# Attention products of the first four output tiles inside the last attention batch, and products four tiles ahead

## The chip, the cores and the metric

One core of a Trainium2 chip. The metric is the device time of one execution, in microseconds (us); three executions of the kernel before took 1540.43, 1540.65 and 1542.9 us.

## The reference

```python
x = L0_attn_x                                   # (8, 512, 1024) float32
x = x + layernorm(attention(layernorm(x)))      # 8 heads of 64, w_qkv, w_o
x = x + layernorm(ffn(layernorm(x)))

def attention(x):
    q, k, v = split(x @ w_qkv.T + b_qkv)
    scores = where(causal, einsum('bhfc,bhtc->bhft', k, q), -10000.0)
    vals = einsum('bhft,bhfc->bhtc', softmax(scores, axis=-2), v)
    return vals @ w_o.T + b_o

def ffn(x):                                     # dense layer and one of four LoRA ranks per row
    scores = x @ gate_w.T + gate_b              # ranks 8, 16, 32, 64; the best one is taken
    return x @ W.T + b + (x @ A[:r].T) @ B[:, :r].T
```

Every product is float32-exact in the kernel: each operand is split into a high part and a rest (names ending in h and l), and three TensorE passes stand for one.

## The kernel before, in words

**Attention phase** (`attention_phase`, L78 to L1143). A loop over the first seven batches of 512 rows, and the last batch written out by the same function with `last=True`. Each batch runs through ten slots (`body`). Slot h has projections of q, k or v after the tables `BETWEEN` and `BETWEEN_LAST` (L105, L118), the scores of head h, the spread of the masked weights of head h-1, the transposes of its probabilities, and the values of head h-2. All engines follow such a slot in their own order, by hand. ACT makes the exponentials and the high parts, DVE the maximum (`scores_max`, L607), the low parts (`p_lo`, L577) and the sum of the values (`vals_sum`, L633), POOL the denominator, the diagonal WT (L461) and the normalised probabilities (`normalise`, L465). SP stores each head's values to memory (`store_vals`, L349); `vals_sum` waits for the store of the head before, since there is one buffer. In the last batch no next batch's projections exist. From slot 5 on, SP loads the output phase's weights: wo (4 chunks), B, wag (8 chunks of 1092 columns); each is split into high (`next_high`, ACT) and low part (`next_low`, DVE; L532, POOL). In slots 8 and 9 TensorE makes the product of output tile 0 (`first_output`, L1069). Its y (`first_attention_out`, L651), scale (L537) and normalised z (L880) follow.

**Output phase** (`output_phase`, L1146 to L1573). A second block with its own semaphores, whose starting values memsets on POOL give (L1308 to L1317). It begins with the product of tile 1, the six wag splits that are left (`late`), the residual x1 and the second layernorm of tile 0, the transposes of its x2n and its x2T parts. Then a loop over the batches, four tiles of 128 rows each. Per tile n on TensorE (L1557): `ffn(n)` (72 matmuls of 364 columns in three banks, the transpose of the routing's result `us` inside the last, 6 matmuls with B), `transpose_x2(n+1)`, `attention_product(n+2)` (24 matmuls of 512 columns; none after the last two tiles). `ffn(n+1)` waits until the three banks of tile n are read (`f_done`, L1534). DVE (L1407): y and statistics of tile n+1, the routing of tile n (L1349, ten small operations), the values' low part, statistics of x1, the low part of x2T, f out of the banks and its statistics. POOL (L1299): scale of y, x1 = x + z (`first_residual`), scale of x1, scale of f, outs = x1 + zf (`second_residual`), all of them in this order. ACT (L1482): the values' high part, z, uT, x2n, x2T's high part, zf.

The few lines on which the order in the output phase rests:

```python
ffn(n)                                   # TensorE, L1560
if more:
    transpose_x2(n + 1)
if not (last and i + 2 > 3):
    attention_product(b, i + 2)
...
layernorm_scale(0, 4 * b + i + 1)        # POOL, L1302
first_residual(b, i + 1)
layernorm_scale(1, 4 * b + i + 1)
layernorm_scale(2, 4 * b + i)
second_residual(b, i)
```

Of the kernel before, what the change touches and what calls it, by code (L numbers as in the profile page):

```python
# [23 lines left out]
P = 128  # L24
# [4 lines left out]
class OutputWeights:  # L29

    def __init__(self, nc, ctx, NB, S, D, PART, R, NAG):
        def sb(name, shape, dt, c=ctx):
            return c.enter_context(nc.sbuf_tensor(name, shape, dt))

        KD, KV = D // P, PART // P
        self.R, self.KV = R, KV
        self.SPLIT_EARLY = 7

        with ExitStack() as early:
            wag_raw = sb("wag_raw", [P, KD, NAG], F32, early)
            wo_raw = sb("wo_raw", [P, KV, D], F32, early)
            B_raw = sb("B_raw", [P, D], F32, early)
        self.wagl = sb("wagl", [P, KD, NAG], F32R)
        self.wol = sb("wol", [P, KV, D], F32R)
        self.Bl = sb("Bl", [P, D], F32R)
        self.wagh = sb("wagh", [P, KD, NAG], F32R)
        self.woh = sb("woh", [P, KV, D], F32R)
        self.Bh = sb("Bh", [P, D], F32R)  # L50
        self.vraw = sb("vraw", [P, 2, PART // P, P], F32)
        self.vh = sb("vh", [P, 2, PART // P, P], F32R)
        self.vl = sb("vl", [P, 2, PART // P, P], F32R)
        self.bo_s = sb("bo_s", [P, D], F32)
        self.y = sb("y", [P, D], F32)
        self.z = sb("z", [P, D], F32)
        self.stats = sb("stats2", [P, 3, 12], F32)
        self.mv = sb("mv2", [P, 3, 2], F32)
        self.var_eps = sb("var_eps2", [P, 3], F32)
        self.rstd = sb("rstd2", [P, 3], F32)  # L60
        self.shift = sb("shift", [P, 3], F32)
        self.xs = sb("xt", [P, 2, D], F32)
        self.floats = 2 * (D // P * NAG + PART // P * D + D) + 3 * 2 * PART + 5 * D
        self.floats += 5 * 64

        self.chunks = [("wo", k, wo_raw[:, k, :], self.woh[:, k, :], self.wol[:, k, :]) for k in range(KV)]
        self.chunks += [("B", 0, B_raw[:, :], self.Bh[:, :], self.Bl[:, :])]
        self.chunks += [("wag", k, wag_raw[:, k, :], self.wagh[:, k, :], self.wagl[:, k, :]) for k in range(KD)]
# [8 lines left out]

def attention_phase(nc, x, wqkvT, bqk, bv, valsT, wl_late, vals_stored, ps_o, W, woT, bo, wagT, BT):  # L78

# [38 lines left out]
    BETWEEN_LAST = BETWEEN[:2] + [([(kind, p, 0, FIRST)], [(kind, p, 0, SECOND)])  # L118
                                  for kind, p in (("k", 2), ("q", 2), ("k", 3), ("q", 3))] + 4 * [([], [])]
# [17 lines left out]
    with ExitStack() as ctx:  # L137
# [6 lines left out]
        wh = sb("wh", [P, KD, E], F32R)  # L144
        wl = sb("wl", [P, KD, 2 * PART], F32R)
# [3 lines left out]
        wl_v_late = sb("wl_v_late", [P, KD - KEPT, PART], F32R)  # L149
        xTh = sb("xTh", [P, KD, S], F32R)  # L150
        xTl = sb("xTl", [P, KD, S], F32R)
        xs = sb("xs", [P, 3, D], F32)

        assert W.floats - D <= 2 * KD * (E + S) + 3 * D
        qst = sb("qst", [P, 2, 2, S], F32R)
        kst = sb("kst", [P, 2, 2, 2, S], F32R)

# [11 lines left out]
        ident = sb("ident", [P, P], F32)  # L169
# [10 lines left out]
        mhalf = sb("mhalf", [P, 1], F32)  # L180
        mone = sb("mone", [P, 1], F32)
        eps = sb("eps", [P, 1], F32)
        hold = sb("hold", [1, 5], F32)
# [67 lines left out]
        tiles_landed = sem("tiles_landed")  # L251
        v_first_landed = sem("v_first_landed")
        v_first_hi = sem("v_first_hi")
        v_first_lo = sem("v_first_lo")
        first_out = sem("first_out")
        first_mv = sem("first_mv")
        first_scale = sem("first_scale")

        LOADS = {5: range(0, 4), 6: range(4, 8), 7: range(8, 11), 8: range(11, 13)}
        SPLITS = {6: range(0, 2), 7: range(2, 4)}
        POOL_SPLITS = range(4, W.SPLIT_EARLY)

        xf = x.rearrange("b s d -> (b s) d")
        vf = valsT.rearrange("b c t -> (b c) t")


        W_CHUNKS = [[k] for k in range(KD)] + [[k, k + 1] for k in range(0, KD, 2)]

        def wh_chunk(n):

            ks = W_CHUNKS[n]
            return wh[:, ks[0], 0:2 * PART] if len(ks) == 1 else wh[:, ks[0]:ks[0] + 2, 2 * PART:3 * PART]
# [51 lines left out]
        def turned(h, place, last):  # L326

            half = None if last else TURNED.get(h, [None] * 3)[place]
            return [] if half is None else [half]

        def between(h, part, b, last):

            return [(kind, p, b + ahead, ks) for kind, p, ahead, ks in (BETWEEN_LAST if last else BETWEEN)[h][part]]

# [3 lines left out]
        def _(sp):  # L338
# [4 lines left out]
            def dup_k(p, b):  # L343

                sp.wait_ge(k_low, 4 * b + p + 1)
                sp.dma_start(kst[HD:P, p % 2, 0, :, :].bitcast(F32), kst[0:HD, p % 2, 0, :, :].bitcast(F32)).then_inc(k_dup[p % 2], 16)
                sp.dma_start(kst[0:HD, p % 2, 1, :, :].bitcast(F32), kst[HD:P, p % 2, 1, :, :].bitcast(F32)).then_inc(k_dup[p % 2], 16)
# [14 lines left out]
            def body(b, last):  # L362
                if not last:

                    sp.wait_ge(k_full, 4 * b + 1)
                    for t in range(3):
                        load_x(t, b + 1)
                for h in range(SLOTS):
                    if h == 2 and not last:

                        sp.wait_ge(v_full, 4 * b + 4)
                        load_x(3, b + 1)
                    if h in (3, 5):
                        dup_k((h + 1) // 2, b)
                    if h in (7, 9) and not last:
# [3 lines left out]
                    if h == 6 and not last:  # L379
# [3 lines left out]
                    if last and h == 5:  # L383
# [1231 lines left out]
```

## Time and profile before

| | |
|---|---|
| median of three executions | 1540.65 us |
| the profiled execution, its own time | 1543.97 us |
| its span, first to last instruction | 1542.1 us |
| busy: PE, DVE, ACT, POOL | 97%, 64%, 45%, 41% |
| mean granted TensorE clock | 0.983 |

A busy share is the time in which an engine had an instruction in work; matmuls overlap one another, so that the distance of two starts tells what one costs. The granted clock is the share of TensorE's full speed that the chip gave in the stretch. Of the span, the attention phase is the first 884 us and the output phase the rest.

### The profile page before, as it was taken

Reading aid. Unit: us, or ns where it says so; the run is one execution under the profiler, and the core shown is the slowest. Engines: PE = TensorE matmul, PEld = TensorE weight load, DVE = VectorE, ACT = ScalarE, POOL = GpSimd, SP = SyncE. Lnnn points to the kernel's source line nnn. Section 1 sums busy time; section 2 is a strip of 40 time slices with the busy share of each in tenths; the row PEclk is TensorE's granted clock in tenths of the full one; section 3 lists DMA queues with packets and bytes.
Section 4 is the critical chain, followed back from the end, with each engine's and each line's share of the span. In section 5 each row is a group of like instructions: output and inputs, shape, how many; then the busy total and the mean of one; then the engine's idle time right before and its main releaser. Section 6 shows DMA issues by size and latency. Waiting matters only on the chain. (4 is left out here: it accounts for less than half of the span.)

```text
span 1542.1 us, 24973 instructions
## 1 busy us (share of the span) xinstructions
PE 1489.6 (97%) x8032; PEld 1313.2 (85%) x8032; DVE 982.4 (64%) x2105; ACT 700.7 (45%) x1499; POOL 626.9 (41%) x1162
## 2 busy tenths in 40 slices
PE   7999999999999999999998689999999999999996
PEld 5888888888888888888887579999999999999996
DVE  7576575664765756756746666666666666666663
ACT  5374474563654655646635633333333333333332
POOL 2253361452543615524513523434444444433433
PEclk9999999999999999999999789999999999999998
DMA  6212113122121131121202612222212222211111
GB/s 232 83 38 82 49 29 90 34 54 75 37 54 61 37 95 34 43 73 37 54 18 73 221 43 69 69 68 68 68 68 68 68 68 68 68 59 56 58 58 41
DMA packets 46926, 102.92 MB, mean 67 GB/s; under 512 B 5040, under 2 KB 21424, under 8 KB 46896
## 3 DMA queue, kind: packets, MB, share of 16 engines
q1 hardware_dynamic: 46896, 102.54, 21.4%
q8 instruction: 16, 0.26, 0.1%
q14 instruction: 14, 0.11, 0.0%
HBM read 60.06 MB, written 25.69 MB: 56 GB/s over the span
## 5 line engine op out<-in xcount | busy, mean ns | idle before, releaser
L1539 PE MATMUL ps_f<-wagh,x2Th 128*128 128x364 f32 x768 | 256.4, 334 | 4.4 <-DVE f L1401 2.9
L1539 PE MATMUL ps_f<-wagl,x2Th 128*128 128x364 f32 x768 | 253.6, 330 | 0.0
L1539 PE MATMUL ps_f<-wagh,x2Tl 128*128 128x364 f32 x768 | 253.1, 330 | 0.0
L973 PE MATMUL ps_o<-xTh,wh 128*128 128x512 f32 x504 | 207.0, 411 | 2.9 <-DVE xTl L562 2.9
L973 PE MATMUL ps_o<-xTh,wl 128*128 128x512 f32 x504 | 198.6, 394 | 0.0
L973 PE MATMUL ps_o<-xTl,wh 128*128 128x512 f32 x504 | 197.8, 392 | 0.0
L1539 PEld LDWEIGHTS ps_f<-wagh,x2Th 128*128 128x128 f32 x768 | 145.5, 189 | 7.2 <-issue 5.0
L1539 PEld LDWEIGHTS ps_f<-wagl,x2Th 128*128 128x128 f32 x768 | 145.5, 189 | 1.3
L1539 PEld LDWEIGHTS ps_f<-wagh,x2Tl 128*128 128x128 f32 x768 | 145.4, 189 | 0.0
L1272 POOL TENSOR_TENSOR var_eps<-mv,eps 128x1 f32<-128x1 f32 x95 | 19.3, 203 | 301.4 <-DVE mv L1335 301.4
L446 POOL TENSOR_TENSOR cw<-wm,cnt 128x4 f32<-128x4 f32 x64 | 12.9, 201 | 307.5 <-ACT pr L808 307.5
L470 POOL TENSOR_SCALAR pr<-pr,rden 128x128 f32<-128x128 f32 (+3 forms) x256 | 137.2, 555 | 0.0
L808 ACT ACTIVATE pr<-ps_s,nm 128x128 f32<-128x128 f32 (+3 forms) x256 | 130.6, 521 | 0.1
L580 DVE TENSOR_TENSOR PTl<-ps_t,PTh 128x512 fp32r<-128x512 f32 (+1 forms) x192 | 110.4, 599 | 23.0 <-ACT PTh L775 19.8
L1440 ACT ACTIVATE zf<-f,shift,rstd 128x512 f32<-128x512 f32 x64 | 48.7, 808 | 164.0 <-POOL shift L1276 164.0
L1386 DVE TENSOR_TENSOR x2Tl<-ps_x,x2Th 128x512 fp32r<-128x512 f32 x64 | 43.8, 692 | 119.2 <-ACT x2Th L1460 118.8
L973 PEld LDWEIGHTS ps_o<-xTh,wl 128*128 128x128 f32 x504 | 95.3, 189 | 21.5
L973 PEld LDWEIGHTS ps_o<-xTh,wh 128*128 128x128 f32 x504 | 95.5, 190 | 19.8 <-DVE xTl L562 3.1
L973 PEld LDWEIGHTS ps_o<-xTl,wh 128*128 128x128 f32 x504 | 95.8, 190 | 17.1
L622 DVE TENSOR_REDUCE nm<-ps_s 128x1 f32<-128x128 f32 (+3 forms) x256 | 107.8, 484 | 2.2
L1518 PE MATMUL ps_o<-woh,vh 128*128 128x512 f32 x248 | 101.3, 408 | 3.9 <-POOL hold L1317 3.9
L775 ACT ACTIVATE PTh<-ps_t 128x512 fp32r<-128x512 f32 (+1 forms) x192 | 94.4, 527 | 21.9 <-PE ps_t L1047 19.9
(175 smaller groups left out, 3527.6 us busy)
## 6 DMA issues: line engine op xcount, KB each, us to landing
kst<-kst SPq DMA_DIRECT2D x64, 256.0 KB, 3.6
xt<-in_x SPq DMA_DIRECT2D x32, 512.0 KB, 4.0
out<-outs SPq DMA_DIRECT2D x32, 512.0 KB, 3.0
xs<-in_x SPq DMA_DIRECT2D x24, 512.0 KB, 4.3
valsT<-vt SPq DMA_DIRECT2D x64, 128.0 KB, 2.3
vraw<-valsT SPq DMA_DIRECT2D x32, 256.0 KB, 4.1
raw<-in_wqkvT SPq DMA_DIRECT2D x12, 512.0 KB, 6.1
wag_raw<-in_wagT SPq DMA_DIRECT2D x8, 546.0 KB, 5.2
```

The source lines that it names most:

```text
L446: pool.tensor_tensor(cw[:, q, :], wm[:, q, :], cnt[:, :], ALU.mult).then_inc(cw_done, 1)
L470: last = pool.tensor_scalar(at, at, rden[:, q, i:i + 1], 1.0, ALU.mult, ALU.mult)
L580: dve.tensor_tensor(PTl[:, o:o + n], ps_t[g % 2][:, 0:n], PTh[:, o:o + n].bitcast(F32), ALU.subtract).then_inc(t_lo, 1)
L622: last = dve.tensor_reduce(nm[:, q, i:i + 1], ps_s[:, S_OFF[i]:S_OFF[i] + (i + 1) * P], AX.X, ALU.max, negate=True)
L775: act.activation(PTh[:, o:o + n], ps_t[g % 2][:, 0:n], ACT.Copy).then_inc(t_hi, 1)
L808: last = act.activation(pr[:, q, S_OFF[i]:S_OFF[i] + n], ps_s[:, S_OFF[i]:S_OFF[i] + n], ACT.Exp, bias=nm[:, q, i:i + 1], accum_out=acc[:, ...
L973: done = pe.matmul(ps[:, :], w[:, k, c:c + P], xT[:, k, :], start=(k == 0 and w is wh and xT is xTh), stop=(k == KD - 1 and w is wl), skip ...
L1272: pool.tensor_tensor(var_eps[:, c:c + 1], mv[:, c, 1:2], eps[:, :], ALU.add)
L1386: dve.tensor_tensor(x2Tl[:, 4 * g:4 * g + 4, :], ps_x[:, g, :].rearrange("p (k t) -> p k t", k=4), x2Th[:, 4 * g:4 * g + 4, :].bitcast(F32 ...
L1440: return act.activation(out_, in_, ACT.Identity, scale=rstd[:, c:c + 1], bias=shift[:, c:c + 1])
L1518: last = pe.matmul(ps_o[:, half, :], a[:, i % 2, k, :], w[:, k, cols], start=(k == 0 and a is vh and w is woh), stop=(k == KV - 1 and a is ...
L1539: last = pe.matmul(ps_f[:, g, 0:GW], a[:, k, :], w[:, k, cols], start=(k == 0 and a is x2Th and w is wagh), stop=False, skip_group_check=True)
```

## The change

The attention phase gets `last_body` functions for every engine, an order by hand for the last batch, in place of `body(NB - 1, True)`:

- the projections of the last batch end in slot 4; slots 5 to 8 hold the attention products of output tiles 0 to 3 (`tile_product`), in the two banks that the projections used;
- y and its statistics for tiles 0 to 2 (`tile_out`), scale, z, x1, second layernorm, transposes and x2T of tile 0 all lie in slots 5 to 9; so do all splits of wo, wag and B;
- the loads of the weights go out earlier: wo after the last v projection, wag, B, bo after the last q projection;
- the memory places of weights and tiles are laid out anew for that, and the semaphores of the output phase exist from the start, with starting values set by POOL at the head of the last batch.

In the output phase TensorE makes the product of tile n+4, DVE y of tile n+3, POOL the scale of y of tile n+3, ACT z of tile n+1 at the head of a tile; y has four buffers. No product stands in the last batch. The opening part of the phase is gone.

```diff
+            def last_body(b):                       # SP
+                sp.wait_ge(v_full, 4 * b + 4)
+                for n in range(W.KV):
+                    load_next(n)
+                for n in range(2):
+                    load_vals(n)
...
+                store_vals(2, b)
+                sp.wait_ge(q_full, 4 * b + 4)
+                sp.dma_start(W.bo_s[:, :], bo.partition_broadcast(P)).then_inc(W.bo_landed, 16)
+                for n in W.wag:
+                    load_next(n)
+                load_next(W.B)
+                sp.wait_ge(s_done, 8 * b + 6)
+                sp.dma_start(W.xs[0][:, :], xf[0:P, :]).then_inc(W.x_landed[0], 16)
+                for h in range(3, NH):
+                    store_vals(h, b)
...
+                for h in range(NH):                 # POOL
+                    if h == 6:
+                        next_low(W.wag[0])
+                        next_low(W.wag[1])
+                        tile_scale(0, 0, 0)
+                    elif h == 7:
+                        tile_residual()
+                        next_low(W.wag[2])
+                    denominator(h, b)
+                    weights(h, b)
+                    diagonal(h, b)
+                    normalise(h, b)
+                tile_scale(1, 4, 0)
+                tile_scale(0, 1, 1)
+                for k in (4, 5, 7):
+                    next_low(W.wag[k])
+                tile_scale(0, 2, 2)
...
+                scores_max(7, b)                    # DVE, slots 7 and 8
+                tile_out(1, 1)
+                tile_vals_low(3)
+                reciprocal(7, b)
+                p_lo(6, 0, b)
+                p_lo(6, 1, b)
+                vals_sum(5, b)
+                tile_statistics()
+                tile_out(2, 0)
+                p_lo(6, 2, b)
+
+                tile_out(2, 1)
+                next_low(W.wag[3])
+                p_lo(7, 0, b)
+                p_lo(7, 1, b)
+                vals_sum(6, b)
+                next_low(W.wag[6])
+                p_lo(7, 2, b)
+                tile_low()
+                next_low(W.B)
+                vals_sum(7, b)
...
+            def tile_product(n, half, ks):          # TensorE
+                if ks[0] == 0:
+                    pe.wait_ge(W.v_ready, n + 1)
+                    if n == 0:
+                        pe.wait_ge(next_lo, W.KV)
+                        pe.wait_ge((k_low, q_low)[half], 4 * NB)
+                    else:
+                        pe.wait_ge(W.y_done, 2 * n - 1 + half)
...
+                for h in range(NH + 1):
+                    if h < len(BETWEEN_LAST):
+                        steps(h, 0, b, True)
+                    else:
+                        tile_product(h - 5, 0, whole)
+                        masked_weights(h - 1, b)
+                    if h >= 2:
+                        values(h - 2, b)
+                    if h >= 1:
+                        transpose_p(h - 1, 0, b)
+                        transpose_p(h - 1, 1, b)
+                    if h < len(BETWEEN_LAST):
+                        steps(h, 1, b, True)
+                    elif h < NH:
+                        tile_product(h - 5, 1, whole)
+                    if h + 1 < NH:
+                        scores(h + 1, b)
+                    if h == NH:
+                        transpose_tile()
+                    if h >= 1:
+                        transpose_p(h - 1, 2, b)
+                tile_product(3, 1, first)
+                values(NH - 1, b)
+                tile_product(3, 1, second)
...
             def body(b, last):                      # output phase, POOL
                 for i in range(4):
                     if not (last and i == 3):
-                        layernorm_scale(0, 4 * b + i + 1)
                         first_residual(b, i + 1)
-                        layernorm_scale(1, 4 * b + i + 1)
-                    layernorm_scale(2, 4 * b + i)
+                    if not (last and i + AHEAD - 1 > 3):
+                        layernorm_scale(0, b, i + AHEAD - 1)
+                    if not (last and i == 3):
+                        layernorm_scale(1, b, i + 1)
+                    layernorm_scale(2, b, i)
                     second_residual(b, i)
...
                     ffn(n)                          # output phase, TensorE
                     if more:
                         transpose_x2(n + 1)
-                    if not (last and i + 2 > 3):
-                        attention_product(b, i + 2)
+                    if not last:
+                        attention_product(b, i + AHEAD)
...
-            attention_product(0, 1)
-            pe.wait_ge(consts, 5)
-            transpose_x2(0)
-            pe.wait_ge(w_ready, len(late))
```

## Rows read from the trace of the kernel before

**Rows 1.** Stretches: start:end, length, each engine's busy us (instructions), granted clock, DMA.
```profile
801.20:840.60 39.40, 38.15 (x207) 32.39 (x205) 23.58 (x56) 22.70 (x61) 10.84 (x26) 1.00 0.15 38
840.60:901.00 60.40, 37.33 (x152) 29.93 (x152) 40.02 (x60) 32.82 (x58) 30.17 (x52) 0.75 0.57 189
901.00:922.50 21.50, 21.50 (x112) 20.37 (x112) 12.61 (x32) 4.35 (x7) 5.31 (x10) 0.90 0.00 1
922.50:1460.00 537.50, 536.04 (x2998) 493.41 (x2997) 352.58 (x811) 177.17 (x270) 218.72 (x351) 1.00 0.20 66
1460.00:1516.90 56.90, 53.87 (x311) 50.37 (x310) 35.68 (x86) 19.06 (x29) 23.52 (x37) 0.99 0.15 51
```

**Rows 2.** Waits of PE, 740 to 960 us: waiting, releaser, total, times, longest.
```profile
PE ps_x L1528 <- ACT x2n L1440: 5.4, 1, 5.4
...
PE ps_o L1518 <- POOL hold L1317: 3.9, 1, 3.9
```

**Rows 3.** Timeline of PE, slot 2: start, duration, engine, line, operation, tiles, shapes, count.
```profile
801.24 0.39 PE L973 MATMUL ps_o<-xTh,wh 128*128 128x512 f32 x1
...
804.14 0.40 PE L1062 MATMUL ps_v<-PTh,v 128*128 128x512 f32 x1
...
805.82 1.04 PE L1047 MATMUL ps_t<-ident,pr 128*128 128x128 f32 x8
...
810.96 0.40 PE L973 MATMUL ps_o<-xTh,wh 128*128 128x512 f32 x1
```

**Rows 4.** Timeline of DVE, 847 to 879 us.
```profile
847.10 0.62 DVE L617 COPY_PREDICATED_SCALAR ps_s<-maskf,masked 128x384 f32 x1
...
849.73 0.17 DVE L627 TENSOR_SCALAR nm<-nm 128x3 f32<-128x3 f32 x1
...
856.10 2.44 DVE L644 TENSOR_TENSOR wol<-wo_raw,woh 128x1024 fp32r<-128x1024 f32 x2
...
877.25 0.68 DVE L657 TENSOR_TENSOR y<-ps_o,bo_s 128x512 f32<-128x512 f32 x1
878.01 0.70 DVE L659 BATCH_NORM_STATS2 stats<-y 128x6 f32<-128x512 f32 x1
```

**Rows 5.** Timeline of POOL, 843 to 882 us.
```profile
843.80 2.06 POOL L470 TENSOR_SCALAR pr<-pr,rden 128x128 f32<-128x128 f32 x4
...
855.07 5.05 POOL L470 TENSOR_SCALAR pr<-pr,rden 128x128 f32<-128x128 f32 x4
...
876.39 5.03 POOL L535 TENSOR_TENSOR wagl<-wag_raw,wagh 128x1092 fp32r<-128x1092 f32 x2
```

**Rows 6.** DMA issues, 838 to 905 us: KB each, median us to landing.
```profile
wo_raw<-in_woT SPq DMA_DIRECT2D x4, 512.0 KB, 7.1
...
valsT<-vt SPq DMA_DIRECT2D x5, 128.0 KB, 2.3
```

**Rows 7.** Timeline of ACT, the uT copies of tiles 0 and 1.
```profile
914.29 0.28 ACT L1473 ACTIVATE uT<-ps_u 128x128 fp32r<-128x128 f32 x1 [7.37 <-PE ps_u L1545]
...
933.78 0.28 ACT L1473 ACTIVATE uT<-ps_u 128x128 fp32r<-128x128 f32 x1 [4.36 <-PE ps_u L1545]
```

**Rows 8.** Timeline of POOL, tile 29: outs and x1.
```profile
1481.23 2.54 POOL L1296 TENSOR_TENSOR outs<-x,zf 128x512 f32<-128x512 f32 x2 [1.00 <-ACT zf L1440]
...
1486.05 2.53 POOL L1287 TENSOR_TENSOR x<-xt,z 128x512 f32<-128x512 f32 x2 [1.00 <-ACT z L1440]
```

**Rows 9.** Timeline of DVE, the routing of tile 0.
```profile
907.22 0.16 DVE L1356 TENSOR_TENSOR scores<-ps_f,gb_s 128x4 f32<-128x4 f32 x1 [3.34 <-PE ps_f L1539]
...
907.70 1.17 DVE L1361 TENSOR_TENSOR tmax<-pmax,scores 128x1 f32<-128x1 f32 x1
...
910.71 0.23 DVE L1374 TENSOR_TENSOR us<-um,us 128x64 fp32r<-128x64 f32 x1
```

**Rows 10.** Timeline of PE, between the last two tiles.
```profile
1512.92 1.03 PE L1528 MATMUL ps_x<-ident,x2n 128*128 128x128 f32 x8
1516.88 0.64 PE L1539 MATMUL ps_f<-wagh,x2Th 128*128 128x364 f32 x1 [2.93 <-DVE f L1401]
```

More of the change, by code:

```diff
@@ L420, in _ @@
             with sp.Fori(0, NB - 1) as b:
[L421 to L425 removed]
+                body(b)
+            last_body(NB - 1)
         @block.gpsimd
@@ L665, in lows, with body @@
+            def lows(h, part, b):
+                for kind, p, row, ks in between(BETWEEN, h, part, b):
                     if ks is not FIRST:
                         {"q": q_lo, "k": k_lo, "v": v_lo}[kind](p, row)
-            def body(b, last):
+            def body(b):
                 for h in range(SLOTS):
-                    if h < NH and (h != BARE + 1 or last):
+                    if h < NH and h != BARE + 1:
                         scores_max(h, b)
-                    if 1 <= h <= 3 and not last:
+                    if 1 <= h <= 3:
@@ L682, in body @@
-                    if h in (BARE, BARE + 1) and not last:
+                    if h in (BARE, BARE + 1):
                         reciprocal(h, b)
@@ L687, in body @@
                         p_lo(h - 1, 1, b)
-                    elif h == BARE + 1 and not last:
+                    elif h == BARE + 1:
                         p_lo(h - 1, 0, b)
@@ new lines, in tile_norm, with tile_high @@
+            def tile_norm(out_, in_, c, row, done):
+                act.wait_ge(W.ln_ready[c], 1)
+                for half in range(2):
+                    cols = slice(PART * half, PART * half + PART)
+                    act.activation(out_[:, cols], in_[:, cols], ACT.Identity, scale=W.rstd[row], bias=W.shift[row])\
+                        .then_inc(done, 1)
+            def tile_high():
+                for g in range(2):
+                    act.wait_ge(W.x2_full, 2 + g + 1)
+                    act.activation(W.x2Th[:, 4 * g:4 * g + 4, :],
+                                   ps_s[:, 512 * g:512 * g + 512].rearrange("p (k t) -> p k t", k=4), ACT.Copy)\
+                        .then_inc(W.x2_hi, 1)
@@ L1009, in scores @@
                     pe.wait_ge(exp_done, H)
-                if h == BEHIND and not last:
+                if behind:
                     pe.wait_ge(x_raw, 8 * b + 5)
@@ L1083, in step, with steps @@
                     project(kind, p, row, ks, last)
-            def steps(h, part, b, last):
-                for n, (kind, p, row, ks) in enumerate(between(h, part, b, last)):
+            def steps(h, part, b, last=False):
+                for n, (kind, p, row, ks) in enumerate(between(BETWEEN_LAST if last else BETWEEN, h, part, b)):
                     here = n == 0 and part == 0 and 1 <= h <= NH and (h != BARE or last)
```

787 lines of the change are left out of this document (455 added, 332 removed).

## The prediction

> **What bounds the kernel now.** I read the page first, then stretches of it cut at the borders of the work, then what TensorE waited for, then the engines' timelines around those waits. TensorE is the bound: in a slot of the attention phase and in an output tile it hardly idles. The exception is the crossing between the phases. From 840.6 to 901.0 us it is busy 37.3 of 60.4 us and its granted clock is 0.75, so part of that time runs at 1.2 instead of 2.4 GHz [rows 1]. In that stretch the projections are used up: heads 6 and 7 alone don't fill TensorE, and then come the end of the block, the second phase's constants, one residual and one layernorm in a row. The longest waits there are 5.4 us for the normalised tile and 3.9 us for the memsets at the start of the second phase [rows 2].
>
> The second thing to see is a small one in each output tile. 27 tiles take 537.5 us [rows 1], 19.91 each, while tiles 0 to 1 are 19.49 apart by their uT copies [rows 7]. No matmul is slower; the two transposes of x2n come late by 0.4 us. Their loop through the other engines takes as long as the period: f out of PSUM, its layernorm, outs, then on POOL the next tile's scale and x1, then its layernorm.
>
> **Step 1, slots 2 to 4 of the last batch.** The same 96 projection matmuls now stand as 36, 36 and 24, where they were 24 in each of slots 2 to 5. Twelve with the mask's matmul take 2.90 us (801.24 to 804.14), so 2.72 without it (384 of its columns against 12 x 512); a whole slot with 24 takes 9.72 (801.24 to 810.96) [rows 3]. So the slots take 12.4 + 12.4 + 9.7 = 34.6 us, and slot 5 begins at 801.2 + 34.6 = 835.8. The splits of wo on ACT and DVE (2.44 us for two on DVE [rows 4]) lie beside them: DVE was busy 23.6 of 39.4 us there [rows 1]. I cost the loads of wo, wag and x at nothing while slots 4 and 5 cover them; see the store in step 2.
>
> **Step 2, slots 5 to 8.** Each gets 24 product matmuls of 512 columns, the work of a projection slot: 9.7 us by TensorE alone, so slot 8 would begin at 864.9. But products 1 to 3 overwrite the bank of the one before, and wait for its y. That add stands on DVE behind a full head. DVE's slot: maximum of the scores 2.8 (847.10 to 849.90), y and statistics of two halves 2 x 1.45 and an aggregate of 0.2, the values' low part 0.6 (half of a wo split), the rest of the head 1.7 (the mean 23.6 / 4 = 5.9 of slots 2 to 5, less the maximum and less 1.4 for a split of q or k, which I put at two operations like y's 0.68): 8.2 us busy [rows 1, 4]. It also waits about 2 us for exps and denominators, so some 10.3 us against 9.7. Slot 7 has the statistics of x1 on top, 2 x 0.7 us. And the store of head 3's values is issued behind about 6 MB of weights; a store lands in 2.3 us, but the four 0.5 MB pieces of wo, issued in a row, took 7.1 [rows 6], so some 0.3 MB per us. Six MB from 835 on need 20 us: the store lands near 856, where DVE wants the buffer at 854. Following the orders of DVE, ACT and POOL I get products 1, 2 and 3 begun late by 0.3, 2.4 and 3.5 us, the third at 869.6. From there TensorE has 2.72 + 0.2 + 1.68 (values, 804.14 to 805.82) + 1.0 (ten transposes) + 0.8 (x2n's eight; 1.04 with the tail) + 2.72 + 1.68 = 10.8 us [rows 3], and waits some 1.7 us for p_lo of head 7, which on DVE stands behind two splits of wag: 882.2. POOL is as late: its normalise of 2.06 us took 5.05 beside DVE splits [rows 5], and after it come two scales of about 1.3 (the 2.3 us between two residuals in [rows 8], less 1 of waiting for z), three splits of 2.5 (5.03 for two [rows 5]) and a third scale: 883.3. The border of the blocks I put at 0.7 us, an estimate well below the wait of 3.9 [rows 2], which also held the end of tile 0's first layernorm and the memsets; both are now inside the last batch. So the first output matmul comes at 884 instead of 901.0, with nothing left ahead of it: **17.0 us**. Bounds: 877.5 if TensorE never waits (864.9 + 10.8 + 1.8 for the last store and the border), 890 if POOL's normalise takes 5 us twice more. I take 884, as DVE's sum is known from rows.
>
> **Step 3, half clock in tile 0.** 901.0 to 922.5 is 21.5 us where an undisturbed tile is 19.49 [rows 1, 7]: 2.0 lost. Before it TensorE had idled 5.4 and 1.5 us; now some 2. Between 0 and 2.0 I take half: **1.0 us**.
>
> **Step 4, products four tiles ahead.** z and the scale of tile n+1 are now ready a tile early. On POOL x1 follows outs at once; before, outs ended at 1483.77 and x1 began at 1486.05 [rows 8], with a scale and the wait for z between. That takes 2.3 us out of a loop of 19.91. It moves x1 onto the routing on DVE, ten small operations: one with two SBUF inputs took 1.17 us beside x1 at 907.70, against 0.16 of the one at 907.22 [rows 9]. With x1's halves of 1.27 us I expect one or two such holds, 1.0 to 1.5 us, as long as the loop passes there. 19.91 - 2.3 + 1.5 = 19.1, under the 19.49 of TensorE, which then sets the pace: 27 x 0.42 = **11.3 us**. Bounds: 0, and 11.3.
>
> The Trainium skill ("SBUF — State Buffer", "Who interferes with whom") says that a VectorE instruction with two SBUF inputs and a GpSimd instruction that reads SBUF block each other for the whole instruction, whichever issued first. By that, the trace agrees: 1.17 us in place of 0.16. Taken at its worst (each routing operation that meets x1 or a scale is held) step 4 would give nothing; that is rival B.
>
> **Step 5, the last tiles.** Now the last four tiles are followed by no product, where it was the last two. Without one, f of tile n must leave its banks before tile n+1 starts: 3.96 us from the transposes to the first matmul (1512.92 to 1516.88, idle 2.93 [rows 10]), and two more such gaps appear. The loop sets the distance of the transposes: 19.91 - 2.3, plus about 1 for the holds and the clock, 18.5. From the start of tile 28 to that of tile 31: 13.2 (19.49 less 2 x 2.75 of the product and 0.8 of transposes) + 18.5 + 18.5 + 4.0 = 54.2, against 56.9 [rows 1]: **2.7 us**. So of the 11.0 us of two products taken out here, 8.3 come back as waits. Bounds: 0 (loop as before) and 5.3 (17.2 by TensorE alone).
>
> **The rest** costs nothing: keep's one memset, the other places of tiles, the transposes of tile 0 moved (in step 2).
>
> **Sum.** 17.0 + 1.0 + 11.3 + 2.7 = 32.0 us. The profiled execution took 1543.97 us, 1542.1 of them span, 3.3 above the median of 1540.65. Its own time less the sum is 1512.0; the median less the sum is **1508.7 us**, which I give.
>
> **Rivals.**
> B: the tile's period stays at 19.9, as the holds on the routing give back the 2.3 us, or another wait has it. For: DVE is busy 352.6 of 537.5 us there [rows 1], and the routing is in the loop. Against: 1.5 us of holds leave 0.4 of margin. Steps 1 to 3 and 5 remain, 20.7 us: 1520.
> C: slots 5 to 8 are bound by DVE and POOL worse than I follow: softmax, y, wag and layernorm feed one another in order, and a slot of 12 us in place of 10.3 to 11 puts the first output matmul at 890 or more. Step 4 stays: 1515 to 1518; with B, 1528.
> D: the crossing goes as TensorE's own sum says (877.5) at full clock: 6.5 and 1.0 us more, with some of step 5's: 1499.
> E, slower than before: the routing, under x1, hands over its result (the tile named us) too late. TensorE transposes that inside the tile, 11.0 us after its start (922.5; its uT copy at 933.78 [rows 1, 7]). The routing begins when 24 of 72 matmuls are done, 4 us into the tile, and took 3.7 us with one hold, 907.22 to 910.94 [rows 9]: it ends at about 8. Further holds beyond 3 us make TensorE wait inside the tile, 31 times; the point from which all 32 us are lost is 1.03 us each, so 4.0 us of holds, three to four of 1.17. At 4.2 us: 1546. Against: x1 has two halves, and each can hold DVE once.
> That the change does not do what it says I exclude by the text of both phases: tile 0's x2 is complete in the first.
>
> The skill ("DMA: Bandwidth & Descriptors", "Queues, rings and completion order") says that each engine takes the descriptors of a ring in order. Only the burst's 7.1 us bear on it here; if the store passed the weights, product 2 would come 1.3 us sooner, less than a term of the range.
>
> **How the numbers follow.** Forecast 0.50; B 0.20; C 0.14, D 0.12, E 0.03; the crossing's gain lost by some unseen wait, 0.01. The forecast's own width is 6 each way, from the bounds of steps 2 and 5. Low end 1498 takes in D; high end 1524 takes in B and most of C; left out are C with B, E, and a little under D. A change of 0.2% (3 us) is about what a measurement here can tell from none. Only E and part of an extreme C fall there: faster 0.95, same 0.02, slower 0.03.
>
> **What would show it.** The first output matmul at 884 with an idle of about 2 us before it; products 2 and 3 waiting for y on DVE by 2 to 4 us; the store of head 3's values landing near 856; clock above 0.9 from 840 to 884. uT copies 19.5 us apart, transposes of x2n without idle before them, the operations of the routing held by x1. Three idle stretches of about 3 us before first matmuls at the end, where there was one. It is wrong if the uT copies stay 19.9 apart (B), if product 3 starts after 876 (C), or if idle time appears before the transpose of that result (E).

## The result, and the profile after

The changed kernel took 1527.03 us (median of 4, 1526.36 to 1529.8) beside 1541.27 us (1540.43 to 1542.9) for the kernel before on the same chip: a ratio of 0.991 (95% interval 0.9893 to 0.9927), 14.2 us. Predicted were 1508.7 us and a range of 1498 to 1524. The change is faster, by less than half of what was forecast, and the time lies 3 us over the range.

The profiled execution has a span of 1525.0 us, 17.1 less than the one of before. Here are its stretches, cut at the same events of the work as [rows 1]: start:end, length, busy us of PE, PEld, DVE, ACT and POOL (instructions), granted clock, DMA share, GB/s.

```profile
801.20:836.90 35.70, 34.69 (x186) 29.64 (x185) 25.40 (x50) 23.69 (x55) 13.28 (x22) 1.00 0.36 107
836.90:896.40 59.50, 44.21 (x223) 36.93 (x221) 43.39 (x74) 33.22 (x69) 36.14 (x47) 0.91 0.41 128
896.40:918.40 22.00, 19.97 (x112) 18.46 (x113) 11.84 (x32) 4.91 (x8) 5.28 (x10) 1.00 0.27 86
918.40:1446.00 527.60, 527.60 (x3000) 495.65 (x2999) 342.76 (x811) 173.31 (x270) 218.43 (x352) 1.00 0.19 67
1446.00:1499.75 53.75, 44.19 (x262) 42.78 (x260) 30.16 (x74) 17.50 (x27) 21.33 (x31) 0.97 0.14 49
1499.75:1525.00 25.25, 14.81 (x79) 14.49 (x79) 6.47 (x22) 3.32 (x5) 7.03 (x10) 0.79 0.10 42
```

Set against the stretches of before, with one correction: the traces of this record differ by some 2 us before DVE's first maximum of the first head (47.3 us in before's, 46.2 in this one), so that piece is taken out.

| stretch | before | after | gain | predicted |
|---|---|---|---|---|
| start to the first scores | 47.3 | 46.2 | 1.1 | 0 |
| first scores to the first output matmul | 853.7 | 850.2 | 3.5 | 17.0 |
| tile 0 | 21.5 | 22.0 | -0.5 | 1.0 |
| tiles 1 to 27 | 537.5 | 527.6 | 9.9 | 11.3 |
| tiles 28 to 30 | 56.9 | 53.75 | 3.1 | 2.7 |
| the last tile to the end | 25.2 | 25.25 | 0.0 | 0 |

The output tiles did what was forecast. 13.5 of the 14.9 us that are missing in the sum are missing in the second line, the crossing. In the fifth stretch, TensorE idles 9.6 of 53.75 us; that is the price of having no product there.

TensorE's waits from 740 to 960 us (waiting, releaser, total, times, longest), against [rows 2]:

```profile
PE ps_o L1351 <- DVE y L747: 9.3, 3, 6.8
PE ps_v L1333 <- DVE PTl L670: 3.5, 1, 3.5
PE ps_x L1785 <- ACT x2n L1708: 2.0, 1, 2.0
PE ps_f L1796 <- PEq L192: 1.6, 1, 1.6
...
```

The wait of 5.4 us for the normalised tile is down to one of 2.0 in the next tile, and the one of 3.9 us for the memsets is gone. Others have come in their place. In the timeline of PE, those of the crossing are the idle times in brackets at the second product half of slot 5, products 2 and 3, the values of head 7 and the first output matmul:

```profile
843.41 0.47 PE L1351 MATMUL ps_o<-woh,vh 128*128 128x512 f32 x1 [0.78 <-DVE qst L677]
865.15 0.77 PE L1351 MATMUL ps_o<-woh,vh 128*128 128x512 f32 x1 [6.84 <-DVE y L747]
878.01 0.47 PE L1351 MATMUL ps_o<-woh,vh 128*128 128x512 f32 x1 [2.21 <-DVE y L747]
890.06 0.80 PE L1333 MATMUL ps_v<-PTh,v 128*128 128x512 f32 x1 [3.50 <-DVE PTl L670]
896.40 0.43 PE L1796 MATMUL ps_f<-wagh,x2Th 128*128 128x364 f32 x1 [1.57 <-PEq L192]
```

A first matmul of 0.77 or 0.80 us instead of 0.47 says one more thing: after the two longest idle times TensorE starts at the lower clock. Of the twelve matmuls from 865.15 on, those from 865.71 to 869.12 start 0.43 us apart, and from 869.45 on they start 0.23 apart again, as at full clock. This half of product 2 takes 4.8 us where one at full clock takes 2.8.

What DVE did meanwhile, in its timeline:

```profile
851.46 1.65 DVE L717 TENSOR_SCALAR nm<-nm 128x3 f32<-128x3 f32 x1
...
863.54 0.74 DVE L728 SCALAR_TENSOR_TENSOR vt<-ps_v,bv_s,vt 64x512 f32<-64x512 f32 x1 [5.22 <-DMA valsT<-vt]
...
880.56 3.10 DVE L734 TENSOR_TENSOR wagl<-wag_raw,wagh 128x1092 fp32r<-128x1092 f32 x1
...
886.08 3.59 DVE L734 TENSOR_TENSOR wagl<-wag_raw,wagh 128x1092 fp32r<-128x1092 f32 x1
...
901.76 0.69 DVE L1622 TENSOR_TENSOR y<-ps_o,bo_s 128x512 f32<-128x512 f32 x1 [6.90 <-DMA gb_s<-in_gb]
```

DVE waits 5.22 us for the store of head 3's values to free its buffer; y of product 1 and so product 2 stand behind it. An operation on 128 by 3 numbers takes 1.65 us where [rows 4] have 0.17. Two splits of wag take 3.10 and 3.59 us, where two of the slightly smaller wo took 2.44 together. And y at the head of the output phase waits 6.90 us for the gate's bias.

SP's queue shows why the store is late: it is issued behind the weights (issue time, duration, count of DMAs):

```profile
834.70 4.03 SPq L404 DMA_DIRECT2D vraw<-valsT  x2
...
839.96 4.50 SPq L401 DMA_DIRECT2D wag_raw<-in_wagT  x8
844.50 1.14 SPq L398 DMA_DIRECT2D B_raw<-in_BT  x2
...
846.98 0.52 SPq L392 DMA_DIRECT2D valsT<-vt  x1
```

### The profile page after: what moved, and what is told of

Its sections match the earlier page's. It is cut to its first block and busy times, and to the rows that moved or that the text cites. A ratio compares the mean times of both kernels' runs of the same rounds, so it can differ in the third digit from the quotient of the medians.

```text
span 1525.0 us, 25023 instructions
## 1 busy us (share of the span) xinstructions
PE 1474.4 (97%) x8032; PEld 1310.3 (86%) x8032; DVE 971.0 (64%) x2103; ACT 696.8 (46%) x1501; POOL 631.7 (41%) x1155
## 3 DMA queue, kind: packets, MB, share of 16 engines
q1 hardware_dynamic: 46896, 102.54, 21.6%
## 5 line engine op out<-in xcount | busy, mean ns | idle before, releaser
L1565 POOL TENSOR_TENSOR small<-small,eps 128x1 f32<-128x1 f32 x92 | 17.4, 190 | 304.8 <-DVE small L1614 304.8
L1708 ACT ACTIVATE zf<-f,small 128x512 f32<-128x512 f32 x64 | 48.7, 809 | 164.6 <-POOL small L1569 164.6
L1740 ACT ACTIVATE uT<-ps_u 128x128 fp32r<-128x128 f32 x32 | 8.9, 277 | 237.7 <-PE ps_u L1802 237.7
L1665 DVE TENSOR_TENSOR x2Tl<-ps_x,x2Th 128x512 fp32r<-128x512 f32 x62 | 40.2, 687 | 119.1 <-ACT x2Th L1729 119.1
```

The source lines that it names most:

```text
L1665: dve.tensor_tensor(x2Tl[:, 4 * g:4 * g + 4, :], ps_x[:, g, :].rearrange("p (k t) -> p k t", k=4), x2Th[:, 4 * g:4 * g + 4, :].bitcast(F32 ...
L1708: return act.activation(out_, in_, ACT.Identity, scale=rstd[r], bias=shift[r])
```

## Experiments

Eleven kernels ran, all edits of the changed kernel. Medians are of four executions where nothing else is said; the kernel before took 1543.12 us beside the first four, 1541.46 beside the next four and 1540.91 beside the last three. Ratios are to these. The changed kernel ran beside 1541.27 us, so a difference in us to it can be off by up to 1.9 us from that source, and a comparison of ratios is the safer one.

**1. The store ahead of the weights.**

```diff
-                for n in W.wag:
+                for n in W.wag[:3]:
                     load_next(n)
-                load_next(W.B)
...
                 for h in range(3, NH):
                     store_vals(h, b)
+                    if h == 3:
+                        for n in W.wag[3:]:
+                            load_next(n)
+                        load_next(W.B)
```

> Edit: only the order on the SP queue. The last five wag chunks and B are loaded after the store of head 3's values instead of before it. Theory Q (the store stands behind six MB of weights): DVE's wait of 5.2 us before the sum of head 4's values is under 0.5 us, product 2 starts near 858 instead of 865.15 and at full clock, the first output matmul comes 7 to 9 us earlier than 896.4; time near 1519. Theory D (DVE's own work is what delays the products): product 2 still starts after 862, time above 1524.

Measured: 1521.89 us, ratio 0.9871 (0.9852 to 0.9889). DVE's wait for the store is gone. TensorE's timeline:

```profile
860.03 0.47 PE L1354 MATMUL ps_o<-woh,vh 128*128 128x512 f32 x1 [1.62 <-DVE y L750]
...
872.85 0.47 PE L1354 MATMUL ps_o<-woh,vh 128*128 128x512 f32 x1 [3.18 <-DVE y L750]
```

Product 2 comes 5.1 us earlier, product 3 5.2, the first output matmul at 889.81 instead of 896.40. So the queue was 5 to 6.5 us of the missing 13.5. It was not all: ahead of product 3 TensorE still waits, 3.18 us here, and DVE's timeline of this kernel shows two holds of the operation on 128 by 3 on the way there:

```profile
851.95 1.22 DVE L720 TENSOR_SCALAR nm<-nm 128x3 f32<-128x3 f32 x1
...
863.54 1.92 DVE L720 TENSOR_SCALAR nm<-nm 128x3 f32<-128x3 f32 x1
```

Both start while POOL splits wag (848.11 for 5.04 us, two in a row, and 862.89 for 2.54) and end at 853.17 and 865.46, when POOL's split in work ends (853.15 and 865.43).

**2. The wait for the bias inside the routing.** One line, `dve.wait_ge(bias_landed, 32)`, moved from ahead of the output phase's loop to the first operation that reads the bias.

> Edit: only the place of DVE's wait for the output phase's two bias loads, which stands ahead of the loop's first y and moves into the routing. Theory W (that wait makes y, routing and x2n of tile 1 late): DVE's idle of 6.9 us at 895 to 902 is gone, TensorE's idle of 2.0 us before the transposes of tile 1 is gone, time 1525. Rival X (the load of x for tile 1, landed at 899.5, sets the end of that chain): y comes earlier but the idle before the transposes stays above 1 us, time 1526.5 to 1527.

Measured: 1524.41 us, 0.9885 (0.9866 to 0.9904). That interval overlaps the changed kernel's, so the trace decides: tile 1's uT copy comes 19.41 us after tile 0's (905.75 to 925.16), where the changed kernel needs 21.84 (907.77 to 929.61), and the wait of 2.0 us ahead of tile 1's transposes is gone. So 2.4 us of tile 0's loss came from one wait placed too early. The clock in tile 0 is 1.00 in both; step 3's reason, half clock, was not what kept the tile long.

**3. The last low part of head 7's probabilities ahead of a split of wag.** On DVE, `p_lo(7, 2, b)` and `next_low(W.wag[6])` change places.

> Edit: only the order on DVE in slot 8; the last low part of head 7's probabilities comes before the split of wag chunk 6 instead of behind it. Theory P (TensorE's wait of 3.5 us before the last values is the path): values of head 7 start near 887 instead of 890.06, and first output matmul moves with it by 3.5 to 4.3 us, time near 1523. Rival L (DVE's splits, held by POOL's three splits to 3.1 and 3.6 us where 1.2 is their length, set the end of the block, whichever comes first): values start near 887, but DVE still ends near 894 and the first output matmul comes only about 1 us earlier, time 1526.

Measured: 1525.42 us, 0.989 (0.9872 to 0.9908), an interval that overlaps the changed kernel's. The wait of the values of head 7 falls from 3.50 to 0.41 us, and 2.5 us of it return at the border:

```profile
886.92 0.51 PE L1333 MATMUL ps_v<-PTh,v 128*128 128x512 f32 x1 [0.41 <-DVE PTl L670]
894.32 0.67 PE L1796 MATMUL ps_f<-wagh,x2Th 128*128 128x364 f32 x1 [4.05 <-PEq L192]
```

DVE's split that was passed still stands ahead of B's and of the last sum of values, and the second phase begins after all of them. The crossing, from the first product matmul to the first output matmul, takes 57.3 us here. That shows no gain: kernels 2, 4 and 5, where this code is untouched, took 57.7, 57.3 and 59.0 us, and the changed kernel 59.5. Changing places inside a queue whose sum is the bound gained nothing that these traces can tell from their spread.

**4. The loop's old order.** POOL's scale of y again ahead of x1, and ACT's z waiting for that scale; everything else as changed.

> Edit: in the output loop alone, POOL makes the scale of the far tile before x1 again, and ACT makes z only when that scale is done; product, y and buffers stay four and three tiles ahead. Theory S (the loop through POOL sets the old period of 19.9 us): the distance of the uT copies goes from 19.53 back to 19.9, 26 tiles lose 9.7 us, and the last tiles some more; time 1537 to 1541. Rival T (the period fell for another reason, such as the memory places or the products' distance): the copies stay 19.5 apart and the time stays at 1527.

Measured: 1536.8 us (ten executions, 1533.38 to 1540.94), 0.9966 (0.9953 to 0.9978). 23 periods from 950.14 to 1405.54 are 19.80 us each. The changed kernel has 19.53, that of before 19.91. So 0.27 of the 0.38 us that a period had gained come back with the old order, which makes the order of POOL and the early z the larger part of step 4's gain; what holds the other 0.11 is open. In time it is 9.8 us by the medians and 8.6 by the ratios. The ten executions spread over 7.6 us, and the profiled one is the fastest of them, only 6.4 us above the changed kernel's.

**5. f out of the banks first.** On DVE, f is added out of its three banks ahead of the low part of the next x2T.

```diff
                         second_layernorm(b, i + 1)
+                    ffn_add(b, i)
+                    if more:
                         x2_low(n + 1)
                     ffn_out(b, i)
```

> The changed kernel with one move on DVE: f is added out of its three banks before the low part of the next tile's x2T, not after it; nothing else. In the last batch, where no product stands between the tiles, the three first ffn matmuls waited 2.92, 2.82 and 2.76 us for f out of the banks. If the low part of x2T that stands ahead of f on DVE is part of that wait (about 1.3 us), each of the three waits falls to some 1.5 us and the stretch from the first matmul of tile 28 to that of tile 31 from 53.8 to about 50 us; over the rest the period stays at 19.53 us, since there f has the whole product to leave the banks. If the low part gates the first matmul as much as f does (it is an operand of it), the wait changes its name only and the time stays within 1 us. The crossing is the same code in both cases: first output matmul at 894 to 897.

Measured: 1517.31 us (1517.0 to 1521.09), 0.9854 (0.9837 to 0.9872): 9.7 us under the changed kernel (8.6 by the ratios), where I had expected about 3.8. More than half was foreseen, the gaps at the end:

```profile
1457.38 0.43 PE L1800 MATMUL ps_f<-wagh,x2Th 128*128 128x364 f32 x1 [1.57 <-DVE x2Tl L1665]
```

The other two are 1.41 us each. In the changed kernel the three are twice as long:

```profile
1462.75 0.41 PE L1796 MATMUL ps_f<-wagh,x2Th 128*128 128x364 f32 x1 [2.92 <-DVE f L1681]
...
1481.35 0.40 PE L1796 MATMUL ps_f<-wagh,x2Th 128*128 128x364 f32 x1 [2.82 <-DVE f L1681]
...
1499.75 0.41 PE L1796 MATMUL ps_f<-wagh,x2Th 128*128 128x364 f32 x1 [2.76 <-DVE f L1681]
```

From the uT copy of tile 28 to that of tile 31, the changed kernel takes 55.61 us and this one 50.16: 5.45 gained. f is out of the banks by the time TensorE has done the transposes (1455.7 and 1455.8); in the changed kernel it was 2.8 us behind them (1462.6 and 1459.8). Its statistics, outs, x1 and the next x2n come earlier with it. The other part was not foreseen: the period itself. The uT copies of tiles 1 and 27, first in the changed kernel, then in this one:

```profile
929.61 0.28 ACT L1740 ACTIVATE uT<-ps_u 128x128 fp32r<-128x128 f32 x1 [7.35 <-PE ps_u L1802]
...
1437.45 0.28 ACT L1740 ACTIVATE uT<-ps_u 128x128 fp32r<-128x128 f32 x1 [7.35 <-PE ps_u L1802]
```

```profile
928.86 0.28 ACT L1744 ACTIVATE uT<-ps_u 128x128 fp32r<-128x128 f32 x1 [8.63 <-PE ps_u L1806]
...
1433.61 0.28 ACT L1744 ACTIVATE uT<-ps_u 128x128 fp32r<-128x128 f32 x1 [8.56 <-PE ps_u L1806]
```

26 periods are 507.84 us there, 19.53 each, and 504.75 here, 19.41: 3.1 us. From the first of the eight transposes of x2n to the product, the changed kernel takes 0.87 to 1.04 us (in before it was 1.04 to 1.12), this one 0.79 in every period. So x2n's second half was still a little late. No wait is listed for it, as the first transpose was on time.

**6 and 7. All four edits, and then the best order.** Kernel 6 has edits 1, 2, 3 and 5. Kernel 7 has also POOL's split of wag 4 in slot 7 in place of the end of the batch, and on DVE `tile_out(2, 0)` ahead of `tile_statistics()`.

> Four edits in one: the loads of wag 3 to 7 and B behind the store of head 3's values (alone: 5 to 6 us), the wait for the gate's bias inside the first routing and not ahead of the loop (2 to 3 us), the last low part of head 7's probabilities ahead of the split of wag 6 on DVE (1 to 2 us), and f out of the banks ahead of x2T's low part (0 to 3 us). If these waits were independent losses the sum is 8 to 13 us under the changed kernel: 1514 to 1519, with the first output matmul at 887 to 889 and tile 1's uT copy 19.5 after tile 0's. If POOL and DVE behind each other are the real limit of the crossing (rival), the edits overlap: the first output matmul stays at 889 to 890, as with the store alone, and the time is 1518 to 1521.

Measured for kernel 6: 1511.4 us (1511.01 to 1512.31), 0.9811 (0.9795 to 0.9827), 15.6 us under the changed kernel. The four edits alone gained 5.1, 2.6, 1.6 and 9.7 us, 19.0 in sum, so 3.4 us are shared; by the ratios it is 21.6 in sum against 15.3. The rival's place for the first output matmul held, and the time was still under the first range, as edit 5 had gained more than I had allowed it. The first output matmul is at 890.47, where the store alone had 889.81, so in the crossing the other edits add nothing to the store; the border has a wait of 2.46 us.

> The kernel of the four edits, with POOL's split of wag 4 moved from the end of the last batch to slot 7, and y's first half of tile 2 on DVE ahead of the statistics of x1. If three splits on POOL at the end, 8.6 us of them beside two on DVE (3.1 and 2.0 to 3.6 us each in place of 1.2), are what holds B's split and so the border, the first output matmul comes 1.5 to 2.5 us earlier than in the kernel of four edits, and product 2 begins without the wait for y (1.6 us): 1512 to 1517. If slots 5 to 8 are bound by POOL itself (rival), the split in slot 7 pushes the denominator and the normalised probabilities of head 7 by 2.5 us, the products come later by that, and the time is the same or 1 to 2 us worse.

Measured for kernel 7: 1509.68 us (1508.09 to 1511.29), 0.9795 (0.9778 to 0.9811), which overlaps kernel 6's interval. The three splits on DVE now take 1.24, 1.28 and 1.21 us, so they stand clear of POOL's. From the first product matmul to the first output matmul it takes 51.9 us, 2.3 less than kernel 6. Product 2's wait of 1.63 us stays, against the expectation.

**8. POOL's splits out of slots 6 and 7.** Edit 1, and the splits of wag 0, 1 and 2 at the end of the batch (two executions).

> The kernel with the store ahead, and POOL's splits of wag 0, 1 and 2 moved out of slots 6 and 7 to the end of the last batch. It tells what those splits cost DVE. If they hold DVE's operation of 128 by 3 elements on the sum of the exponentials' maxima (1.22 and 1.92 us measured beside them, 0.17 without), both come back to 0.17 to 0.2 us, product 2 begins about 1.2 us and product 3 some 3 us earlier than with the store ahead alone (859 and 870 in place of 860.0 and 872.9). If the holds come from something else (rival), they stay at over 1 us. The end of the batch is longer in either case, since six splits stand there on POOL: first output matmul at 895 or later, 1527 to 1533 us in all.

Measured: 1522.63 us. DVE's and TensorE's timelines:

```profile
851.78 0.17 DVE L717 TENSOR_SCALAR nm<-nm 128x3 f32<-128x3 f32 x1
...
862.32 0.17 DVE L717 TENSOR_SCALAR nm<-nm 128x3 f32<-128x3 f32 x1
```

```profile
858.80 0.47 PE L1351 MATMUL ps_o<-woh,vh 128*128 128x512 f32 x1 [1.54 <-DVE y L747]
...
869.87 0.47 PE L1351 MATMUL ps_o<-woh,vh 128*128 128x512 f32 x1 [2.33 <-DVE y L747]
```

Both holds are gone, and products 2 and 3 come where they were expected (859, 870). The end came better than expected: the first output matmul at 891.80, after a wait of 5.0 us at the border, since six splits of POOL in a row took 18.00 us and ended at 889.8. The whole is 4 us under the range I had given.

**9, 10 and 11. Two ways out of the hold.** Kernel 9 is kernel 7 with each of POOL's splits as two operations of 546 columns. Kernel 10 is kernel 7 with DVE's operation in another form; kernel 11 has both.

```diff
-                dve.tensor_scalar(nm[:, q, 0:3], nm[:, q, 0:3], -MASKED, None, ALU.min).then_inc(nm_ready, 1)
+                dve.tensor_reduce(nm[:, q, 0:3], nmx[:, q, :, :], AX.X, ALU.min).then_inc(nm_ready, 1)
```

`nmx` holds each negated maximum beside the constant 10000, written once.

> The best kernel so far (1509.68 us), with each of POOL's splits of wag as two operations of 546 columns in place of one of 1092. If DVE's small operation waits for the end of the POOL operation in work, its holds of 1.23 and 1.94 us become at most 1.3 and on average 0.7 us, products 1 and 3 begin some 0.5 to 1 us earlier each, and the whole is 0.5 to 2 us faster: 1508 to 1509. If it waits until POOL has no further such operation queued (rival), the holds stay at 1.2 and 1.9 us and the time stays within 0.5 us, or rises a little for three more instructions on POOL.

Measured: 1506.9 us (1506.17 to 1509.95), 0.9775 (0.9758 to 0.9793). The operation takes 0.21 and 0.77 us instead of 1.23 and 1.94. Not all of the gain is the holds': product 3 runs at full clock throughout in this trace, its matmuls 0.23 us apart, while in the traces of kernels 7 and 10 seven of the distances are 0.42 or 0.43. From the start of product 3 to the last values it takes 8.9 us here and 10.5 in both of those. What the shorter holds give is 1.3 us up to product 3 (34.3 us after product 0, against 35.6 in kernel 7).

> The best kernel so far, with the minimum of the negated maxima and 10000 on DVE (128 by 3 elements) written as a reduction over pairs (maximum, constant) in place of a tensor_scalar; POOL's splits stay where they are. If the hold hangs on the form of DVE's operation, as it did not touch reductions and statistics beside POOL's splits in any trace so far, the operation takes 0.2 us in all heads, the wait of 1.0 us ahead of product 1's second half and the 1.75 us ahead of product 3 shrink by 1.0 and up to 1.2 us, the first output matmul comes 1 to 2.5 us earlier: 1507 to 1509. If every DVE operation on SBUF is held (rival), it takes 1.2 and 1.9 us as before and the time stays the same.

Measured: 1506.32 us (1505.66 to 1506.88), 0.9774 (0.9756 to 0.9791), the lowest median of all; the intervals of kernels 7, 9, 10 and 11 overlap, so the traces have to tell what each edit did. The operation in the changed kernel and in this one, over all 64 heads (ns least, median, most):

```profile
L717 DVE TENSOR_SCALAR nm<-nm x64: 169/170/1648, 47.9 to 868.7; 128x3 f32<-128x3 f32 x64
```

```profile
L725 DVE TENSOR_REDUCE nm<-nmx x64: 158/159/162, 47.0 to 859.9; 128x3 f32<-128x6 f32 x64
```

Two of those 64 stand beside POOL's splits as before (849.37 beside splits from 845.52 to 850.59, 859.90 beside one from 859.26 on), and none is held. Product 3 begins 34.1 us after product 0, 1.5 us sooner than in kernel 7. There is a gain that I had not counted: from this operation in the first head to the first product matmul, this kernel takes 787.1 us (47.0 to 834.14) and the changed one 789.0 (47.9 to 836.92). The other batches had small holds too: 22 of these operations took 0.35 to 0.75 us, in the changed kernel and likewise in the one before (0.37 to 0.75). The expected shrinking of the wait ahead of product 3 did not come: it stays at 1.75 us.

> Both edits: POOL's splits in halves, and the minimum as a reduction. What is left of holds are DVE's own splits and low parts beside POOL's. If the two edits act on the same holds, the time is that of the reduction alone within 0.5 us: 1507 to 1509. If halves also free the values' low part (1.45 us measured, 0.64 without POOL beside it), it is up to 0.5 us better than either.

Measured: 1507.43 us (1504.61 to 1508.75), 0.9774 (0.9757 to 0.9792). The two act on the same holds: both together are within 1.2 us of each alone.

From the first product matmul to the first output matmul, the term of step 2, the kernels take the times below. They are of one trace each. The changed kernel and kernels 2, 4 and 5 have the same code here and spread from 57.3 to 59.5 us, so a difference of 2 us in this table is not shown by it alone.

| kernel | us |
|---|---|
| changed | 59.5 |
| same code in the crossing (2, 4, 5) | 57.7, 57.3, 59.0 |
| low part's place (3) | 57.3 |
| store ahead (1) | 53.0 |
| store ahead, POOL's splits late (8) | 55.5 |
| four edits (6) | 54.2 |
| best order (7) | 51.9 |
| with halves (9) | 49.4 |
| with the reduction (10) | 50.4 |
| with both (11) | 51.2 |
| predicted for the changed kernel | 48.2 |

## Why the prediction was right or wrong

**Step 1** was small and a little short. The slots took 12.51, 13.73 and 9.79 us against 12.4, 12.4 and 9.7. One wait of 1.01 us for q's low part on DVE is new in slot 3. With 0.8 us lost before slot 2, for which I have no cause, slot 5 began 2.2 us later than forecast when both are counted from the first scores.

**Step 2** failed, and with it the forecast: 59.5 us from product 0 to the first output matmul in place of 48.2. The wait for the store was named and sized at 2 of its 5.2 us; the holds of DVE by POOL's splits of wag had no term at all. Up to product 3 I had 33.8 us, and it took 41.1:

- *The store.* I had it landing near 856, wanted at 854: 2 us. It freed the buffer at 863.54, wanted at 858.3: 5.22 us. I counted 6 MB from 835 on at 0.3 MB per us. But SP was held for 4.03 us at the loads of the values, so that the weights went out from 839.96, and the 5.9 MB (eight pieces of wag, B, bo and x) took until 863.5, 0.25 MB per us by that count. The wait has a second price that I had not counted: 1.9 us of lower clock in the half product behind it. With the store ahead, product 3 comes after 36.0 us.
- *The holds.* I did charge holds to the routing, and to POOL's normalise in a bound, but none to the softmax's operation on 128 by 3, because [rows 4] show it at 0.17 us, beside no split on POOL. The same trace has 22 of it at 0.37 to 0.75 us in earlier batches, and I had not looked. It took 1.65 us in slot 6 of the changed kernel, and 1.22 and 1.92 in slots 6 and 7 with the store ahead. With neither the store's wait nor these holds, product 3 comes after 33.5 us (836.35 to 869.87 in experiment 8), where I had put it. There TensorE's waits are 0.78, 1.54 and 2.33 us, 4.65 in sum. My sum needs 4.7 between 864.9 and 869.6, though its text says 3.5 for product 3; the two do not fit each other, and the larger is the one that the sum uses.

From product 3 to TensorE's end I had 12.6 us, and it took 16.8. I took the splits of wag on DVE at their free price. Three of POOL's splits stand beside the two of DVE, and each of DVE's became 3.1 to 3.6 us. The wait of 3.50 us ahead of the last values, where I had 1.7, is not the measure of it: kernels 1, 2, 4 and 5 wait 1.94 to 1.98 us there, and the values still begin 12.05 or 12.06 us after product 3 in each of them, as in the changed kernel, since TensorE ran slower on the way. What counts is that distance, and in the changed kernel alone 1.4 us of lower clock behind the longer wait. In kernel 6, with the low part ahead of the split, the stretch is 15.0 us, and in kernel 7, where one split of POOL also lies elsewhere, 13.8.

The border I had at 0.7 us after POOL's end; the second phase begins 1.5 us after DVE's last operation, in kernels 7, 9 and 10 alike. From TensorE's end it is 1.6 us in the changed kernel where I had 1.8, so nothing of the miss lies there.

**Step 3** had the wrong cause. The clock in tile 0 is 1.00, better than expected, yet the tile took 22.0 us: the wait for the gate's bias ahead of the loop stands on DVE ahead of the statistics of x1, so x2n of tile 1 came late. The prediction has no such wait. It is a term that was missing, 2.4 us (experiment 2), and without it tile 0 takes 19.4.

**Step 4** was right. POOL's x1 follows outs at once, and two operations of the routing are held, for 1.9 us together (1.00 and 1.18 against 0.16 each), where I had 1.0 to 1.5. POOL first, then DVE:

```profile
1212.74 2.54 POOL L1588 TENSOR_TENSOR outs<-x,zf 128x512 f32<-128x512 f32 x2 [1.00 <-ACT zf L1708]
1215.44 2.54 POOL L1579 TENSOR_TENSOR x<-xt,z 128x512 f32<-128x512 f32 x2 [0.16 <-POOL outs L1588]
```

```profile
1215.75 1.00 DVE L1638 TENSOR_TENSOR pmax<-scores 128x2 f32<-128x2 f32 x1
1216.82 1.18 DVE L1640 TENSOR_TENSOR tmax<-pmax,scores 128x1 f32<-128x1 f32 x1
```

The period is 19.53 against a forecast of 19.49; rival B's 19.9 did not come. But 19.49 was not TensorE's own pace, as I had called it: experiment 5 ran at 19.41, with the transposes at 0.79 us in every period.

**Step 5** was right in kind and size: 3.1 us against 2.7, with three gaps of 2.8 to 2.9 us where 3 us were forecast.

**The rivals.** C, the slots bound by DVE and POOL, with a first output matmul at 890 or more, is what happened in the crossing (896.4); I priced it at 1515 to 1518, since I took 890 as its place and not its start. Its 12.4 us over 884 and the 1.5 of tile 0 lead from 1508.7 to 1522.6, most of the way to what was measured. I gave it 0.14, as nearly every price on DVE and POOL was that of an operation alone. The condition I had set for it, product 3 after 876, came (878.0). B, D and E did not happen.

The Trainium skill ("SBUF — State Buffer", "Who interferes with whom") names `tensor_scalar` among the operations that can take the port pair shared with GpSimd, in its two-port modes, and says that `tensor_reduce` never contends on trn2. The traces agree: the one form took 1.22 to 1.94 us beside a split (kernels 1 and 7), the other 162 ns at most (kernel 10). I had drawn on the page's rule for two inputs only, and so looked for holds in the routing and not in the softmax.

## What to carry to other kernels

Work that is moved beside other work has to be priced beside it: list for each moved operation of GpSimd which VectorE operations it will overlap, the tiny ones on the path above all. A transfer's start follows from what its queue waits for first, and a small store that frees a buffer goes ahead of large loads that nobody wants yet. A wait placed once ahead of a loop is free only while something ahead of it is slower.

## What the runs showed of the hardware

- Beside a GpSimd operation of 2.5 us, a VectorE `tensor_scalar` on 128 by 3 numbers took 1.22 to 1.94 us instead of 0.17; as `tensor_reduce` it took 0.16 there.
- Where both engines had splits with two SBUF inputs in work, both lost: VectorE's took 2.0 to 3.6 us in place of 1.2, and six of GpSimd's took 18.00 us, 2.49 to 3.59 each, in place of 2.5 (kernels 1 and 8).
- After an idle time of 6.84 us (granted clock 0.81 in the stretch that holds it), TensorE ran most of twelve matmuls at the 1.2 GHz level, 0.43 us apart in place of 0.23. The first matmul does not tell the whole: after 3.18 us it took 0.47 us in the kernel with the store ahead, and 0.77 in kernel 6, and in the first of these the matmuls from 0.6 us later on were 0.43 apart too. After the same 1.75 us, product 3 fell to the lower level in kernels 7 and 10 and stayed at full clock in kernel 9: idle times of this length can go either way.
- A store of 128 KB, issued behind 5.9 MB of loads in the same queue, set its buffer free 16.5 us after its issue; with only bo, three pieces of wag and x ahead of it, 2.7 MB, nobody waited for it.
